# Second attention: the third maxima unit moved out of the products with values, and those moved behind the subtracting fills

## What is computed

```
qkv = x @ W_qkv.T                      # 16 heads of 16, 512 tokens, 4 batches
attn = einsum('bhqd,bhkd->bhqk', q, k) * SCALE
attn = where(causal, attn, -inf)
probs = softmax(attn)
out = einsum('bhqk,bhkd->bhqd', probs, v)
return out @ W_proj.T
```

## Time and profile before

| | |
|---|---|
| Time, median of 3 runs (lowest, highest) | 1039.01 us (1037.42, 1040.25) |
| Span of the profiled execution | 1038.3 us |
| PE busy | 957.4 us (92%) |
| DVE, ACT, POOL busy | 605.2, 495.7, 434.4 us |
| First attention, main loop | about 30 to 260 us |
| Second attention, main loop | about 585 to 822 us |
| Mean granted TensorE clock | 0.957 |

### The profile page before, as it was taken

The page is one execution under the profiler, slowest core; times in us unless marked ns, Lnnn a source line. Parts: engine busy times, 40 slices in busy tenths (PEclk is TensorE's granted clock), DMA queues, the critical chain, the costliest instruction groups (busy, mean ns, idle before and its releaser), DMA issues. The chain is left out here.

```text
span 1038.3 us, 17900 instructions
## 1 busy us (share of the span) xinstructions
PE 957.4 (92%) x6076; PEld 766.7 (74%) x6076; DVE 605.2 (58%) x1972; ACT 495.7 (48%) x897; POOL 434.4 (42%) x410
## 2 busy tenths in 40 slices
PE   7899999997789999999992989999999789999997
PEld 5566766675589999999992656676767478888886
DVE  6677787877524444444444687786676235454535
ACT  7356556665104443433347265656666444333332
POOL 4453444425623223322336544554253544524233
PEclk9899999998889999999996899999999979999999
DMA  5443222201232333233104752624321010202111
GB/s 191 146 162 129 70 72 92 72 22 36 81 132 80 121 131 123 100 131 131 66 20 134 240 185 87 209 77 144 121 62 31 1 52 1 93 22 92 60 54 41
DMA packets 51968, 98.95 MB, mean 95 GB/s; under 512 B 7579, under 2 KB 23835, under 8 KB 51766
## 3 DMA queue, kind: packets, MB, share of 16 engines
q1 hardware_dynamic: 48822, 89.62, 25.5%
q0 software_dynamic: 3072, 8.39, 2.5%
HBM read 61.63 MB, written 36.36 MB: 94 GB/s over the span
## 5 line engine op out<-in xcount | busy, mean ns | idle before, releaser
L864 ACT ACTIVATE a_probs<-a_ps_b 128x512 f32<-128x512 f32 x320 | 187.7, 603 | 112.3 <-PE a_ps_b L936 109.8
L1181 DVE CUSTOM_DVE_ANT_0 a_masked_s<-a_ps_a,a_mask_f 128x512 f32<-128x512 f32 (+1 forms) x256 | 153.4, 620 | 83.2 <-PE a_ps_a L920 78.9
L920 PE MATMUL a_ps_a<-a_k_st,a_q_st 128*128 128x256 f32 (+3 forms) x512 | 191.6, 421 | 10.5 <-DVE a_nmax L1181 6.0
L529 POOL TENSOR_SCALAR_AFFINE_SELECT a_probs<-a_probs 128x512 f32<-128x512 f32 x128 | 80.5, 644 | 160.7 <-ACT a_probs L864 160.6
L920 PEld LDWEIGHTS a_ps_a<-a_k_st,a_q_st 128*128 128x128 f32 x512 | 95.9, 198 | 59.2 <-DVE a_nmax L1181 31.1
L936 PE MATMUL a_ps_b<-a_q_less,a_k_st 128*128 128x384 f32 (+3 forms) x512 | 134.0, 325 | 3.9 <-ACT a_probs L864 3.1
L1927 PE MATMUL exp_ps_o<-w_both,exp_h_hi 128*128 128x512 f32 x320 | 115.5, 402 | 0.0
L936 PEld LDWEIGHTS a_ps_b<-a_q_less,a_k_st 128*128 128x128 f32 x512 | 89.2, 192 | 29.4 <-ACT a_probs L864 18.3
L1845 ACT ACTIVATE exp_h_hi<-exp_ps_u 128x320 fp32r<-128x320 f32 x128 | 54.3, 438 | 87.2 <-PE exp_ps_u L1910 87.2
L2075 POOL TENSOR_TENSOR dense_h_lo<-dense_mixed,dense_h_hi 128x512 fp32r<-128x512 f32 x40 | 53.1, 1328 | 101.7 <-ACT dense_h_hi L2140 101.7
L1884 DVE SCALAR_TENSOR_TENSOR exp_h_lo<-exp_ps_u,exp_h_hi 128x320 fp32r<-128x320 f32 x128 | 61.4, 490 | 56.3 <-ACT exp_h_hi L1845 55.4
(11 more groups left out here) (290 smaller groups left out, 2127.4 us busy)
## 6 DMA issues: line engine op xcount, KB each, us to landing
w_raw<-in_m_w SPq DMA_DIRECT2D x16, 1024.0 KB, 5.6
scratch<-a_hi SPq DMA_DIRECT2D x24, 512.0 KB, 3.0
dense_mix_rows<-mix_rows SPq DMA_DIRECT2D x9, 768.0 KB, 6.3
scratch<-a_lo SPq DMA_DIRECT2D x24, 256.0 KB, 3.2
a_q_st<-scratch SPq DMA_DIRECT2D x64, 96.0 KB, 2.2
a_k_st<-scratch SPq DMA_DIRECT2D x64, 96.0 KB, 2.4
exp_rows<-dispatched SPq DMA_DIRECT2D x9, 640.0 KB, 3.9
dispatched<-kept_sub SPq DMA_DIRECT2D x9, 512.0 KB, 2.9
```

Of the source, the lines that this page charges most:

```text
L529: nc.gpsimd.affine_select(out=blocks, in_=blocks, compare_op=ALU.is_ge, fill=0.0, base=0, pattern=[[0, HPG], [1, P]], channel_multiplier=- ...
L864: nc.scalar.activation(probs[:, k, :], ps_b[k % B_BANKS][:, :], ACT.Exp, scale=scale).then_inc(exps, 1)
L920: last = nc.tensor.matmul(ps[:, at:at + wd], q_st[t % STACKS][:, h // PER_TILE, i * P:wd], k_st[t % STACKS][:, h, 0:wd], start=True, stop= ...
L1181: nc.vector.tensor_tensor_reduce(masked_s[n % 2][:, 0:wd], ps[:, 0:wd], mask_f[:, SEQ - wd:SEQ], -1.0, -NEG, ALU.add, ALU.min, nmax[:, t % ...
```

## The change

The call of `max_unit(t + 2, 2)` inside `values_of_old` goes, and so does the call of `values_of_old` (and, in the rounds that have no old step, of `max_unit(T, 2)`) in slot 1 of the second attention. `max_unit` is issued in every slot, 2 included, and `values_of_old` is called in slot 2 behind the fills in both attentions. In round 0 the twelve transposes of `turn_identity` now come behind `max_unit(0, 2)` in slot 2. No other engine's instructions change.

```
@@ -1046,8 +1046,6 @@
                 pe.wait_ge(masked, t * 4 + 1)
                 need(pe, pv_copied, t)
                 pv(t, 0).then_inc(pv_done, 1)
-                if not rope and t + 2 < STEPS:
-                    max_unit(t + 2, 2)
                 pe.wait_ge(masked, t * 4 + 3)
                 pv(t, 1)
                 pv(t, 3).then_inc(pv_done, 1)
@@ -1091,20 +1089,14 @@
                             elif rope and T in (1, 2):
                                 pe.wait_ge(ones_in, T * HPG)
                             pe.wait_ge(stacked[T % STACKS], 16 * HPG * (2 * (T // STACKS + 1) - (T % STACKS == 0)))
-                        if rope or s != 2:
-                            max_unit(T, s)
-                        elif T == 0:
+                        max_unit(T, s)
+                        if not rope and (T, s) == (0, 2):
                             turn_identity(nc, ps_b[1], ident, 12)
                     if prob_at(T, s):
                         prob_unit(*prob_at(T, s))
-                    if not rope and s == 1:
-                        if 0 <= T - 2 < STEPS:
-                            values_of_old(T - 2)
-                        elif T < STEPS:
-                            max_unit(T, 2)
                     for name, half in FILLS_AT.get((T, s), ()):
                         fill(name, half)
-                    if rope and s == 2 and 0 <= T - 2 < STEPS:
+                    if s == 2 and 0 <= T - 2 < STEPS:
                         values_of_old(T - 2)
                     if s == 5 and 0 <= T - 2 < STEPS:
                         pe.wait_ge(masked, (T - 2) * 4 + 4)
```

## The result

The changed kernel is slower: median 1043.76 us of 17 runs (1037.39 to 1047.74) against 1038.51 us of 17 runs of the kernel before (1035.76 to 1041.95), 5.25 us between the medians. The ratio of the two sets is 1.0037 with a 95% interval of 1.0020 to 1.0054, that is 3.8 us (2.1 to 5.6); the means lie 4.0 us apart. The two measures differ because the times of the changed kernel fall into two groups, and its median is the lowest time of the upper one. Two later comparisons, each with its own runs of the kernel before beside it, gave 1.0061 (1.0038 to 1.0085) and 1.0041 (1.0016 to 1.0067).

A forecast was written before the change was run, and what follows sets the result against it. TensorE was taken to bound the second attention, busy 201.4 of 207.0 us. Waits of +6.05 less gains of 2.25 gave +3.8 us, step 16 -0.8, total +3.0: median 1042.0 us, range 1037.5 to 1045.5.

The forecast's parts named there:

- (a): Second attention, TensorE switches between product and matmul modes: 3.77 us instead of 4.21, 0.36 us gained per step without wait.
- (b): First less fill waits for VectorE's maxima in seven steps of the second attention, 0.29 to 2.08 us each.
- R2: Rival: the waits vanish because VectorE gains as well; 1033.2 us, faster; chance 0.08 together with R4.
- (d): Second attention: less fills evacuated early, ScalarE's first exponential starts sooner; 0.1 us in each of four light steps, -0.4.
- (c): Second less fill waits for its PSUM bank: 0.21 us in steps 2, 6, 10; 0.26 + 0.08 in 5, 9.
- (e): Step 16 of the second attention: less fills start inside the wait for POOL's mask; 0.8 us gained.
- the nearer row: Step 16 case where the clock falls again after the pause; products end at about 812.0, 0.5 us gained.
- my other end: Step 16 case where the clock does not fall again: 1.9 us gained.
- R3: Rival: clock falls in long waits of steps 2, 3, 13; one or two falls give 1043.7 to 1045.4; chance 0.17.
- against it: Argument against R3: TensorE is dense around steps 3 and 13, its stalls at clock 1.00; step 16 has half the work.
- R1: Rival: waits mostly repaid by VectorE and ScalarE slack; halving the three large terms gives +0.8, 1039.8 us; chance 0.15.
- R4: Rival: both less fills stay behind the products, only the break goes; 1036 us; chance 0.08 together with R2.

The follow-up runs named there:

- the kernel with the break removed: Changed kernel with the products with values kept unbroken but ahead of the less fills; ratios to the kernel before 0.9939 and 0.9946.
- the kernel with the busy waits: Changed kernel plus 4 to 14 idle transposes ahead of the first less fill in steps 2, 3, 6, 7, 13, 14; ratio to the kernel before 1.0012.
- third profile: The changed kernel, unedited, profiled a third time (its second repetition); ratio to the kernel before 1.0041.
- the control: Kernel before, with the second attention's less fills reading the identity without waiting, maxima not subtracted; ratio to the unedited kernel before 1.0006.

## Why the prediction was right or wrong

The time, 1043.8 us, lies in the range. The likeliest time of 1042.0 was 1.8 us too low; of the difference to the kernel before, +3.0 was forecast and +5.25 came (by the medians), and the 0.5 us by which the base of three runs lay too high hides a part of that. The measured 0.37% has an interval that spans the 0.3% that I had put it just inside of. The waits and their cause were read rightly. The sum of the steps came out too high and the clock, which the forecast put at nothing, makes up for more than that; that the total is so near is in part luck.

(a) Switches: predicted 3.77 us from p9 to m3 and 0.36 us of gain up to p0; measured 3.77 and 0.36 in steps 4, 11 and 15, and 0.27 in steps 8 and 12, those without margin. The estimate that put a price on the drain of the Trainium skill, "TensorEngine Tiling (Array Packing)", section Tiling Modes, was 0.30, too low for those three.

(b) The waits of n0: predicted 1.77, 2.08, 1.01, 1.35, 0.29, 1.85 and 0.68 us; measured 1.77, 2.07, 1.02, 1.35, 0.30, 1.85 and 0.67. They could be read so well from the trace of before because neither p9 nor L1206 hangs on the moved instructions; this holds also against R2.

Net of everything, by the starts of p9 and p0 where the clock is full:

| Step | Predicted | Measured | Of it by p0 | Of it by the next p9 |
|---|---|---|---|---|
| 2 | +0.55 | 0.0 | +1.80 | -1.79 |
| 3 | +1.8 | +1.7 | +1.78 | -0.06 |
| 6 | +0.5 | +0.1 | +1.04 | -0.98 |
| 7 | +1.1 | +1.0 | +1.08 | -0.09 |
| 10 | +0.3 | +0.2 | +0.31 | -0.07 |
| 13 | +1.5 | +1.4 | +1.48 | -0.07 |
| 14 | +0.3 | +0.2 | +0.28 | -0.10 |
| 4, 5, 8, 9, 11, 12, 15 | -1.8 | -2.2 | -1.6 | -0.6 |
| ScalarE's head start (d) | -0.4 | in the last column | | |
| Sum | +3.8 | +2.4 | | |

The stretch from step 2's p9 to step 16's became 3.1 us longer, 2.4 of it the table's and 0.7 the fall in step 2; 4 was named as the sign. Steps 2 and 6 were the mis-sized terms of this part: I had VectorE 0.5 us late from m3 on, and for good. It is late at m3 by that much (it idles 0.56 us in front of it), and makes it up again. (d) came out at 0.06 to 0.10 in nearly every step, some 1 us in all, but not where I had put it. p2 waited for no exponential before: in step 4 there is no idle time from p0 on in either kernel. The whole of it lies between p0 and the instruction behind it, 0.31 us before (643.98 to 644.29) and 0.24 after. Before, p0 starts 0.15 us behind ScalarE's evacuation of n0 (3.74 to 4.32 us behind p9), so it had just been waiting for it; after, and in the kernel with the break removed, that evacuation is done earlier, and p0 is followed in 0.24 us in both.

(c) The waits of n1 came as predicted (steps 2, 5, 6, 9 and 10; step 5 and 9 keep a gain of 0.1 together with the next p9).

(e) Step 16: the clock fell again, as the nearer row said.

```profile
809.88 0.63 PE L949 MATMUL a_ps_m<-a_identr,a_nm 128*128 128x128 f32 x4 [1.57 <-DVE a_nm L1198]
...
811.50 3.46 PE L960 MATMUL a_ps_pv<-a_probs,a_v 128*32 128x512 f32 x24
814.89 0.73 PE L936 MATMUL a_ps_b<-a_q_less,a_k_st 128*128 128x512 f32 x2
```

The products took 3.46 us, p9 to p0 7.08 instead of 7.34: 0.3 us gained. In the kernel with the busy waits the clock didn't fall there, and the same stretch took 5.46. Against 7.34 that looks like the 1.9 of my other end, but it sets a stretch without a fall against one with it; against the 5.81 of the kernel before without a fall it is 0.35. So the order is worth 0.3 us either way, and I had taken 0.8. The rest of my 1.9 was the fall in the profile that I read. Whether it comes differs: behind this step's pause it came in two of five profiles with the wait ahead of V1, and in six of seven with the wait ahead of n0.

R3, the clock: I gave it 0.17 as a rival, with falls in one or two of the long waits. It is no rival but a part of the result. With the falls in the three profiles (net 0.7 us in the first, 5.4 in the second, 3.2 in the third; per fall 0.7 in step 2, 1.7 to 3.1 in step 3, 1.6 in step 13) the mean is 3.1 us. 2.4 - 0.3 + 3.1 = 5.2 us, beside 3.8, 6.4 and 4.3 us by the three ratios (1.7 to 9.0 by their intervals). Three profiles don't fix the last term, and the clock of all the runs gave 1.7 to 3.4. The step that failed is the "against it" of R3: that TensorE is dense around these steps does not keep the clock up, if the pause itself is 1.6 to 1.9 us. My bound of 1.7 us for a fall was right for a fall of 3.4 us; in one profile it lasted 6.8 in step 3 and cost 3.1.

R1, the waits repaid: true in steps 2 and 6 entirely, in the others not. R2, the waits vanishing, and R4, another order, were excluded by the trace.

So the sum of the steps was 1.4 us too high (3.8 for 2.4; with step 16 0.9, 3.0 for 2.1), and the clock, put at 0, by 1.7 to 3.4 too low. "No granted clock under 1.00 between 598 and 805 us" was named as a sign against the forecast, and it is the one that failed: 0.99 there, with a stretch of 0.50.

## What to carry to other kernels

Before work is moved out of the space between two dependent steps, ask what that work covered: here a part worth 6 us came together with one that cost 10 to 13, and each showed its size only when measured alone. The time at which another engine's signal comes can be read from the trace before, step by step, if it doesn't hang on what is moved; then the new wait is a difference of two rows. A pause of TensorE of 1 to 2 us can cost more than its own length, since low clock may follow (here 0.7 to 3.1 us a fall, behind six of nine pauses of 1.6 to 1.9), so allow for as much again, or put the smallest piece of real work into it. And before a stage is compared between two profiles, look whether its clock was the same in both: step 16 differs by 1.5 us between two executions of one kernel.

## What was not expected of the hardware

The clock first. A pause of 1.58 us was already followed by low clock in step 16 of one profile of the kernel before, and a pause of 1.59 in the same place was not in the other. After the change the idle times of 1.6, 1.9 and 1.6 us in steps 2, 3 and 13 were followed by 3.4 to 6.8 us at half clock in six of the nine cases of three profiles. With the same instructions and the same waits, which of them it is differs from execution to execution; what decides it, no run here shows. Shorter ones can do it too. In step 13 of the first attention, which the change doesn't touch, n0 waits 0.99 us behind four small products; low clock followed in 7 of the 12 profiles that have this wait, and in none of the two whose edit took it away. Here is one of the seven (the changed kernel, third profile):

```profile
200.54 0.63 PE L949 MATMUL a_ps_m<-a_identr,a_nm 128*128 128x128 f32 x4 [0.99 <-DVE a_nm L1198]
...
202.65 2.82 PE L960 MATMUL a_ps_pv<-a_probs,a_v 128*32 128x512 f32 x24
```

The products took 2.82 us there, for 1.93 at full clock. And in the control (the kernel before with the identity) the clock fell once in step 2, behind five idle times of 0.3 to 0.5 us within 8 us, with no long one; it did so in the kernel with the products first in both attentions too, while both profiles of the kernel before have the same five without a fall. So I can't give a length from which it happens.

The second is how VectorE made up for its late start in step 2. First POOL and VectorE in the kernel before, then in the changed one (third profile). L1381 is there what L1389 is before:

```profile
617.21 1.55 POOL L683 TENSOR_TENSOR w_gate_lo<-a_wide_raw,w_gate_hi 128x640 fp32r<-128x640 f32 x1
...
617.75 1.30 DVE L1389 SCALAR_TENSOR_TENSOR kept_x<-kept_sub,a_c_inv,kept_x 128x256 f32<-128x256 f32 x1
...
618.73 1.73 POOL L683 TENSOR_TENSOR w_up_lo<-a_wide_raw,w_up_hi 128x640 fp32r<-128x640 f32 x1
...
622.34 0.47 DVE L1389 SCALAR_TENSOR_TENSOR kept_x<-kept_sub,a_c_inv,kept_x 128x256 f32<-128x256 f32 x1
```

```profile
615.57 1.55 POOL L683 TENSOR_TENSOR w_gate_lo<-a_wide_raw,w_gate_hi 128x640 fp32r<-128x640 f32 x1
...
616.75 0.65 DVE L1381 SCALAR_TENSOR_TENSOR kept_x<-kept_sub,a_c_inv,kept_x 128x256 f32<-128x256 f32 x1
...
617.08 1.74 POOL L683 TENSOR_TENSOR w_up_lo<-a_wide_raw,w_up_hi 128x640 fp32r<-128x640 f32 x1
...
617.80 1.31 DVE L1381 SCALAR_TENSOR_TENSOR kept_x<-kept_sub,a_c_inv,kept_x 128x256 f32<-128x256 f32 x1
```

The same SCALAR_TENSOR_TENSOR, with two inputs in SBUF, takes 0.47 us alone (622.34). Beside POOL's L683 it takes 1.30 (617.75): L683 ends at 618.76, and it ends 0.29 later. In the changed kernel it starts at 616.75, when the first L683 has only 0.37 us to run (to 617.12), and again ends 0.28 us behind that, after 0.65 us; the next one, beside the second L683 (to 618.82), ends 0.29 behind it. So a VectorE that comes 0.6 us later against POOL waits 0.65 less for it. That is what repaid step 2; in step 6 the same instruction, started 0.9 us later behind p9, took 0.48 instead of 1.30. The Trainium skill, "SBUF — State Buffer", section "Who interferes with whom", has a rule for it: the port pair that VectorE and GpSimd share is an exclusive lock, and a VectorE instruction with two inputs in SBUF contends for it with a GpSimd instruction that reads SBUF; the order of issue decides who waits. The rows agree in all three cases: the length is not stretched in proportion, it runs to the end of L683 plus a constant. No experiment was made on this by itself; it is read from two traces, and the lengths of POOL's instructions in a profile are rough.
